# State loop, routing and experts of a two-layer AdaLN kernel: another order, another operand, other loads

## What is computed

```python
def layer0_mixer(u):                         # chunked state space model
    z, x, B, C, dt = split(layer_norm(u) @ in_proj_w.T)
    y = ssd_chunked(x, dA, B, C, chunk) + x * D
    return u + (y * silu(z)) @ out_proj_w.T

def layer0_moe(x):                           # E=64, K=8, CAP=64, H=256, I=96
    w, sel = top_k(softmax(x @ gate_w.T), K) # w is then divided by its sum
    pos = cumsum(one_hot(eid)) ...           # place of a token in its expert
    inp = zeros(E, CAP, H).at[eid, pos].set(x[tok])   # if pos < CAP
    h = silu(inp @ wg) * (inp @ wu)
    out = h @ wd
    return sum over K of out[eid, pos] * w
```

## Time and profile before

| | |
|---|---|
| median of 3 runs | 800.57 us (797.09 to 804.24) |
| the profiled execution, span | 801.1 us |
| busy | PE 77%, DVE 63%, ACT 35%, POOL 31% |
| chain that ended last | PE 53%, DVE 21%, issue 8%, ACT 8%, DMA 6% |
| DMA | 62.83 MB, mean 78 GB/s |

### The profile page before, as it was taken

The page is one execution under the profiler, slowest core; times in us unless marked ns, Lnnn a source line. Parts: engine busy times, 40 slices in busy tenths (PEclk is TensorE's granted clock), DMA queues, the critical chain, the costliest instruction groups (busy, mean ns, idle before and its releaser), DMA issues.

```text
span 801.1 us, 9617 instructions
## 1 busy us (share of the span) xinstructions
PE 620.3 (77%) x3248; PEld 469.8 (59%) x3248; DVE 508.0 (63%) x1121; ACT 283.7 (35%) x887; POOL 249.7 (31%) x288
## 2 busy tenths in 40 slices
PE   2997988740109789975385898898988789998996
PEld 0544766530008677763163665666666668887885
DVE  5547567833997536724677789889757636655444
ACT  2644544400103222332255665646646431111110
POOL 1228003275650000137545255251101126640000
PEclk9999999965559956987577999999999999999999
DMA  8900001049017996863112043150000000000000
GB/s 317 351 1 0 1 2 47 34 147 299 3 42 205 278 281 222 244 195 98 45 48 49 5 54 37 17 53 1 0 1 1 1 0 1 1 1 27 1 1 27
DMA packets 29808, 62.83 MB, mean 78 GB/s; under 512 B 5827, under 2 KB 13297, under 8 KB 29184
## 3 DMA queue, kind: packets, MB, share of 16 engines
q1 hardware_dynamic: 22336, 45.42, 18.1%
q0 software_dynamic: 7424, 16.80, 9.3%
HBM read 48.56 MB, written 17.83 MB: 83 GB/s over the span
## 4 chain that ended last, share of the span: by engine, by line
PE 53%; DVE 21%; issue 8%; ACT 8%; DMA 6%; POOL 2%; another core or an unknown queue 1%; SPq 1%; POOLq 0%; DVEq 0%; ACTq 0%
PE bank L1104 47%; DMA arena<-expert_in 4%; DVE arena L1054 2%; POOL expert_in L396 2%; ACT arena L594 2%; DVE arena L1013 2%; PE bank L1326 2%; PE bank L1444 1%; DVE arena L968 1%; DMA expert_out<-arena 1%; PE bank L1272 1%; ACT arena L612 1%; DMA arena<-in_wmod 1%; DVE arena L1002 1%
## 5 line engine op out<-in xcount | busy, mean ns | idle before, releaser
L1104 PE MATMUL bank<-arena 128*96 128x64 f32 (+9 forms) x2040 | 425.2, 367 | 64.0 <-issue 26.0
L1104 PEld LDWEIGHTS bank<-arena 128*128 128x128 f32 (+4 forms) x2040 | 295.3, 192 | 160.6 <-issue 100.9
L396 POOL DMA_INDIRECT expert_in<-arena x64 | 65.2, 1019 | 88.7 <-DVE arena L857 70.1
L410 POOL DMA_INDIRECT arena<-expert_out,arena x64 | 72.6, 1134 | 19.0 <-issue 18.5
L692 ACT ACTIVATE arena<-bank 128x512 f32<-128x512 f32 x32 | 19.1, 598 | 112.4 <-PE bank L1104 112.4
L1085 DVE TENSOR_TENSOR arena<-arena,bank 128x512 f32<-128x512 f32 x32 | 22.0, 687 | 56.1 <-ACT arena L692 56.1
L594 ACT ACTIVATE arena<-bank,arena 128x128 f32<-128x128 f32 x128 | 45.2, 383 | 25.2 <-DVE arena L1006 25.2
L1104 PE MATMUL bank<-h_hi,gu_hi 128*128 128x512 f32 x128 | 50.8, 397 | 0.5 <-ACT arena L695 0.5
L1104 PE MATMUL bank<-h_low,gu_hi 128*128 128x512 f32 x128 | 50.5, 394 | 0.0
L1104 PE MATMUL bank<-h_hi,low 128*128 128x512 f32 x128 | 50.1, 391 | 0.0
L434 POOL TENSOR_TENSOR low<-arena,gu_hi 128x128 fp32r<-128x128 f32 x64 | 29.7, 495 | 60.4 <-DVE dn_hi L1017 60.4
(11 more groups left out here) (200 smaller groups left out, 1024.2 us busy)
## 6 DMA issues: line engine op xcount, KB each, us to landing
arena<-in_wgu SPq DMA_DIRECT2D x32, 384.0 KB, 6.5
arena<-in_wd SPq DMA_DIRECT2D x32, 192.0 KB, 8.9
expert_in<-arena SPq DMA_DIRECT2D x1, 4096.0 KB, 23.9
arena<-expert_in SPq DMA_DIRECT2D x16, 256.0 KB, 7.2
expert_out<-arena POOLq DMA_DIRECT2D x16, 256.0 KB, 6.5
arena<-in_w SPq DMA_DIRECT2D x1, 2048.0 KB, 9.3
arena<-in_wmod SPq DMA_DIRECT2D x1, 1536.0 KB, 15.0
arena<-in_w_in SPq DMA_DIRECT2D x1, 1288.0 KB, 8.8
```

What stands on the lines that cost most here:

```text
L396: pool.indirect_dma_start(xin, bass.IndirectOffsetOnAxis(scatter8[:, t, k:k + 1], 0), h[:, t, :], None, bounds_check=SLOTS - 1, oob_is_err ...
L410: pool.indirect_dma_start(gath[t % 2][:, k, :], None, yex, bass.IndirectOffsetOnAxis(gather8[:, t, k:k + 1], 0), bounds_check=SLOTS - 1, o ...
L1104: return pe.matmul(o, lhsT, rhs, start=start, stop=stop, **kw)
```

## The change

- **Turns.** The state loop and its routing have T+2 = 10 turns. Turn s routes tile s-2 whole: its transposes stand first in PE's turn (L1257's counterpart), then `cs_rows` and G, then its logits; DVE and ACT take them in the same turn, and the place multiplications close PE's turn, in `bank5`. There are no batches; `choose` and `place_rows` lose the normalisation of the weights, which is done once for all tiles behind the loop.
- **Fewer operations on DVE.** POOL multiplies `w_out` by the gate row once, so x gains tile by tile in one addition. The scale and shift of the experts' input leave DVE: ACT applies them by partition as it copies the transposed tile (two operations) and the transposed expert rows (two a group); four transposes ahead of the loop make the columns (`h2_cols`). What is scattered is the normalised row.
- **Loads.** Pairs 0 to 10 and 12 load one or two a turn inside the loop, as `st_mm` and `yT_mm` reach a turn; pair 11 and one set of codes behind it. z and x of a tile stand side by side so that slots come free. `load_rows` moves from SP's queue to POOL's, between the stores.
- **Experts.** The rows are the stationary side, 64 columns, and gate and up weights, 192 columns, move past them; two experts fill the two halves of a bank's partitions. The hidden tile is then transposed (`hidden_T`, two more transposes a group) and copied by ACT. Three output buffers instead of two, each of 128 partitions, one copy a group.
- **Decoding** a half set of codes takes 4 operations on DVE instead of 7; the pace is 1.5 halves a group instead of 1.25.
- **Gathers.** Two tiles are gathered ahead of the first attention turn instead of three, and behind L425 of tile t stands `gather(t + 2)` instead of `gather(t + 3)`.

```diff
-            for q in range(4):
+            for q, tile, early in ((0, 1, True), (1, 2, True), (2, 2, True), (3, 3, True), (6, 3, True), (12, 4, True), (4, 1, False),
+                                   (5, 2, False), (7, 4, False), (8, 5, False), (9, 6, False), (10, 7, False)):
+                sp.wait_ge(st_mm if early else yT_mm, tile)
                 load_pair(q)
             sp.wait_ge(yT_mm, T)
-            load_codes(0)
-            load_codes(1)
-            for q in range(4, NS):
-                load_pair(q)
-            for n in range(2, NEARLY):
+            load_pair(11)
+            for n in range(NEARLY):
                 load_codes(n)
...
+            pool.wait_ge(ld_wout, 16)
+            pool.tensor_tensor(w_out_s, w_out_s, under(mod[0][:, 2, :], 4), ALU.mult).then_inc(wout_ready, 1)
...
+            def load_rows(g):
+
+                if g >= NX:
+                    pool.wait_ge(xgT_mm, g - NX + 1)
+                pool.dma_start(xg[g % NX], xin[4 * CAP * g:4 * CAP * (g + 1), :].rearrange("(q p) c -> p q c", p=P))\
+                    .then_inc(xg_loaded[g % NX], 16)
+
+            pool.wait_ge(scattered, 16 * T * TOPK)
+            for g in range(NX):
+                load_rows(g)
             for g in range(NG):
...
+                if g + NX < NG:
+                    load_rows(g + NX)
+                pool.wait_ge(ob_ready, g + 1)
+                pool.dma_start(yex[4 * CAP * g:4 * CAP * (g + 1), :].rearrange("(q p) c -> p q c", p=P), ob[g % 3])\
+                    .then_inc(ob_stored[g % 3], 16)
+
+            for i in range(3):
+                pool.wait_ge(ob_stored[i], 16 * len(range(i, NG, 3)))
...
-            for t in range(3):
-                gather(t)
+            gather(0)
+            gather(1)
...
-                if t + 3 < T:
-                    gather(t + 3)
+                if t + 2 < T:
+                    gather(t + 2)
...
-            for s in range(T + 4):
+            for s in range(T + 2):
+                if 0 <= s - 2:
+                    less_maximum(s - 2)
                 if s < T - 1:
                     state_after(s)
-                if 0 <= s - 3 < T:
-                    less_maximum(s - 3)
+                if 0 <= s - 2:
+                    choose(s - 2)
                 if s + 1 < T:
                     make_M(s + 1)
+
+                if 0 <= s - 1 < T:
+                    t = s - 1
+                    dve.wait_ge(o_mm, t + 1)
+                    dve.wait_ge(xh_ready, t + 1)
+                    dve.tensor_tensor(x[:, t, :], x[:, t, :], bank[7][:, 0:DM], ALU.add).then_inc(x1_ready, 1)
+                    dve.wait_ge(x1_ready, t + 1)
+                    moments(x[:, t, :], t, mv[2]).then_inc(var_ready, 1)
 
                 if s < T:
                     dve.wait_ge(Yd_mm, s + 1)
...
                 if 0 <= s - 1 < T:
                     t = s - 1
-                    dve.wait_ge(o_mm, t + 1)
-                    dve.wait_ge(xh_ready, t + 1)
-                    link(dve.tensor_tensor(h[:, t, :], bank[7][:, 0:DM], mod[0][:, 2, :], ALU.mult))
-                    dve.tensor_tensor(x[:, t, :], x[:, t, :], h[:, t, :], ALU.add).then_inc(x1_ready, 1)
-                    dve.wait_ge(x1_ready, t + 1)
-                    moments(x[:, t, :], t, mv[2]).then_inc(var2_ready, 1)
-                if s - 4 in LAST:
-                    place_rows(LAST.index(s - 4))
-                if s - 3 in LAST:
-                    choose(LAST.index(s - 3))
-
-                if 0 <= s - 1 < T:
-                    t = s - 1
-                    dve.wait_ge(rstd2_ready, t + 1)
-                    link(normed(h[:, t, :], x[:, t, :], t, mv[2], rstd[2]))
-                    link(dve.tensor_tensor(h[:, t, :], h[:, t, :], mod[0][:, 4, :], ALU.mult))
-                    dve.tensor_tensor(h[:, t, :], h[:, t, :], mod[0][:, 3, :], ALU.add).then_inc(h2_ready, 1)
-
+                    dve.wait_ge(rstd_ready, 1 + T + t + 1)
+                    normed(h[:, t, :], x[:, t, :], t, mv[2], rstd[2]).then_inc(h2_ready, 1)
+                if 0 <= s - 2:
+                    place_rows(s - 2)
...
+            for s in range(T + 2):
+                if 0 <= s - 2:
+                    t = s - 2
+                    pe.wait_ge(h2_ready, t + 1)
+                    pe.wait_ge(yT_ready, t + 1)
+                    for j in range(KC):
+                        ins = pe.transpose(bank[6][:, j * P:(j + 1) * P], h[:, t, j * P:(j + 1) * P], ident)
+                    ins.then_inc(rowsT_mm, 1)
                 if s + 1 < T:
                     cs_rows(s + 1)
+                    pe.wait_ge(M_ready, s + 1)
+                    mm(bank[2][:, 0:P], bT[:, s + 1, :], cT[:, s + 1, :]).then_inc(G_mm, 1)
+                if 0 <= s - 2:
+                    t = s - 2
+                    if t == 0:
+                        pe.wait_ge(ld_gate, 16)
+                    pe.wait_ge(rowsT_ready, 2 * T + 2 * t + 2)
...
                         pe.wait_ge(xdec_ready, s + 1)
                         if s >= 1:
                             pe.wait_ge(state_ready, s)
+                        if s >= 3:
+                            pe.wait_ge(place_read, s - 2)
                         mm(bank[5][:, :], bn[:, s, :], xdec[s]).then_inc(st_mm, 1)
                     if s >= 1:
                         pe.wait_ge(state_ready, s)
                         if s >= 2:
                             pe.wait_ge(yo_ready, s - 1)
                         mm(bank[4][:, :], cT[:, s, :], state[:, s % 2, :]).then_inc(Yo_mm, 1)
-                    if s >= 1:
-                        pe.wait_ge(y_ready, s)
-                    pe.wait_ge(xD_ready, s + 1)
-                    mm(bank[3][:, :], ident, xD[s], start=True, stop=False, skip_group_check=True)
-                    places(s)
-                    if s + 1 < T:
-                        pe.wait_ge(M_ready, s + 1)
...
-                    pe.wait_ge(M_ready, s + 1)
-                    for i in range(H):
-                        ins = mm(bank[3][:, i * HD:(i + 1) * HD], Lm[:, s % 2, i * P:(i + 1) * P], xs[:, s, i * HD:(i + 1) * HD],
-                                 start=False, stop=True, skip_group_check=True)
-                    ins.then_inc(Yd_mm, 1)
                 if 0 <= s - 1 < T:
                     t = s - 1
                     pe.wait_ge(y_ready, t + 1)
-                    if t >= 2:
-                        pe.wait_ge(h2T_ready, t - 1)
-                        pe.wait_ge(lmax_ready, t - 1)
+                    if t >= 1:
+                        pe.wait_ge(lmax_ready, t)
                     for j in range(4):
                         ins = pe.transpose(bank[6][:, j * P:(j + 1) * P], zs[:, t, j * P:(j + 1) * P], ident)
                     ins.then_inc(yT_mm, 1)
+                if s < T:
+                    pe.wait_ge(xD_ready, s + 1)
+                    mm(bank[3][:, :], ident, xD[s], start=True, stop=False, skip_group_check=True)
+                if 0 <= s - 1 < T:
+                    t = s - 1
                     if t == 0:
-                        pe.wait_ge(ld_wout, 16)
+                        pe.wait_ge(wout_ready, 1)
                     pe.wait_ge(yT_ready, t + 1)
                     if t >= 1:
                         pe.wait_ge(x1_ready, t)
                     for j in range(4):
                         ins = mm(bank[7][:, 0:DM], yT[:, t % 2, j * P:(j + 1) * P], w_out_s[:, j, :], start=j == 0, stop=j == 3)
                     ins.then_inc(o_mm, 1)
-                if 0 <= s - 2 < T:
+                if s < T:
+                    pe.wait_ge(M_ready, s + 1)
+                    for i in range(H):
+                        ins = mm(bank[3][:, i * HD:(i + 1) * HD], Lm[:, s % 2, i * P:(i + 1) * P], xs[:, s, i * HD:(i + 1) * HD],
+                                 start=False, stop=True, skip_group_check=True)
+                    ins.then_inc(Yd_mm, 1)
+                if 0 <= s - 2:
                     t = s - 2
-                    pe.wait_ge(h2_ready, t + 1)
+                    pe.wait_ge(mask_ready, t + 1)
+                    pe.wait_ge(state_ready, min(s + 1, T - 1))
                     if t >= 1:
-                        pe.wait_ge(lmax_ready, t)
...
+                        pe.wait_ge(place_read, t)
+                    mm(bank[5][:, 0:E], strict_b, mask_b[:, t, :], stop=False)
+                    mm(bank[5][:, 0:E], ones_b, run_b[:, t, :], start=False).then_inc(pos_mm, 1)
...
             def gate_up(g):
-                pe.wait_ge(xgT_ready, g + 1)
+                pe.wait_ge(xgT_ready, 2 * (g + 1))
                 if g >= 2:
                     pe.wait_ge(hid_ready, g - 1)
-                for e in range(4):
-                    q = 2 * g + e // 2
-                    if e % 2 == 0:
-                        pe.wait_ge(w_loaded[q % NS], 32 * (q // NS + 1))
-                    w = wgu_s[q % NS][:, e % 2, :].rearrange("p (a j f) -> p a j f", a=2, j=KC)
-                    for a in range(2):
-                        for j in range(KC):
```

(31 more changed lines are left out.)

331 lines of the change are left out of this document (144 added, 187 removed).

## The result

The changed kernel takes 829.76 us in the median (827.72 to 830.09) against 802.4 (four runs of the kernel before): 1.0358 times the time of before, 95% interval 1.0297 to 1.042. It is slower by 3.6%. The forecast was 778, with a range of 755 to 806. The profiled execution spans 827.5 us, 26.4 more than before.

The account below looks back on a forecast made before the run. PE bounds the state loop, one chain through all engines the routing tail, DMA the experts, DVE attention. 801.1 - 33.2 (earlier experts) - 20.9 (experts and output) + 31.9 (attention) = 778.9, less 0.5: 778 us, range 755 to 806.

Parts of the forecast that it names:

- the last takes 1.0, and DVE may start 1.9 later: Attention: gathered rows ready about 14.0 us after the rotary operation starts; DVE's waits cost +31.9 us in all.
- Turn: 11.42 - 1.16 + 1.8 = 12.06 us: State loop: two waits for ACT go, a 1.8 us wait for the norm comes; bounds 11.4 and 12.6.
- the slow rival: State loop: PE's clock falls to half behind the new wait, +10 us a turn, up to 850 us; chance 0.12.
- `Yd` of turn 1: State loop: PE's last long work of turn 1 was to end at 93.9 us, 90.7 in the kernel before.
- I take 5.0: Experts: PE's time per group taken as 5.0 us, 83 us in 16 groups.
- take 86 us: Experts: DMA needs 86 us for the stage's own 25.3 MB at 294 GB/s.
- side by side: Experts: both partition halves run at once, PE's group 2.9 us, stage on the DMA floor, 771 us; chance 0.10.
- lose about 3 us before the first `down` frees slots: Experts: DMA loses about 3 us early in the stage, from its start at 203.
- With 2 us of stalls: Experts: PE ends at 296 with 2 us of stalls, giving a stage of 90.3 us, 17.3 less.
- Rows on POOL's queue: Experts: rows from POOL's queue would overtake weights, so PE's 4.36 us wait would go; the sum did not use it.
- The third output buffer, -3.6: End of experts: the last copy's wait goes; gathers begin 5.3 us after PE's end instead of 8.9.
- two turns less: Tail of routing: one part of the -33.2 us by which the experts start earlier.

Follow-up runs that it names:

- a_one_half: a_swap_e with both experts of a pair written to the same half of the bank's partitions, half the expert outputs missing; 831.34 us, one run.
- a_swap_e: The changed kernel with the two inner loops of gate and up exchanged, both chunks of one expert first; 821.97 us, one run.
- a_codes2: The changed kernel with two sets of codes decoded ahead instead of one and 1.25 half sets a group instead of 1.5; 823.82 us.
- a_codes3: The changed kernel with a third buffer for codes, three sets loaded right behind the loop; 823.84 us.
- a_codes_scratch: a_codes3 with later code sets loaded into a buffer nothing reads, DVE decoding the first two sets again and again; 822.09 us.
- a_late_loads: The changed kernel with all 13 pairs of weights loaded behind the loop in one burst; 830.36 us.
- a_gather3: The changed kernel with three tiles gathered ahead of attention and gather(t + 3) again, as in the kernel before; 769.79 us.
- a_norm_first: The changed kernel with DVE's norm of the routed tile moved ahead of y in each loop turn; 812.60 us.
- a_fill: The changed kernel with five useless multiplications in PE's wait at the head of turns 2 to 7; 820.06 us.
- b_gather2: The kernel before with only the gathers changed: two tiles ahead, gather(t + 2); 862.18 us, 1.083 of before.

## Why the prediction was wrong, step by step

**Attention, "the last takes 1.0, and DVE may start 1.9 later".** The mechanism, the place and the number of turns were right, the term was mis-sized: +52.5 us over the turns instead of 26.8. The rows come 17.6 us after the rotary operation's start (522.61 to 540.24), not 14.0: 2.6 of the 3.6 us are the landing, 4.5 instead of 1.9, and 1.0 is the pace on POOL, 10.6 us from the first gather's start to the last's where the sum had 9.25 and some 0.3 for DVE. Both terms came from the head of attention, where DVE stands idle; they were used in the middle of a turn. The kernel before has that case too, hidden there, since nobody waits for it. Its DMA view from 499 to 509 (a digit for the busy tenths of each quarter microsecond):

```profile
DMA  9018928915918909950692000000000000000000
```

POOL's last gather of that turn starts at 499.92 and takes 1.00, and DMA is busy until 504.5: 3.6 us behind its end, and 16.8 behind L425's start at 487.74. With 16.8 the sum would have had 2.8 us more for each of five turns, 14 of the 25.7. The Trainium skill (Perfetto Trace Analysis, DMA Instruction — SWDGE (GPSIMD)) says that such an instruction ends in the profile when its descriptors are written, not when the data has moved; the rows agree, with 1.9 and 4.5 us between the two. The second part of the miss is PE's clock: behind 10.6 us of idle PE's first four multiplications take 3.75 us at clock 0.50, and POOL's rotary operation starts 17.4 us after `maxima` instead of 16.2; that the one makes the other is argued and not tested. Also, one turn of before was 29.0 us and not 31.2 (the prediction took one for all), which alone is 2 us.

**The loop, "Turn: 11.42 - 1.16 + 1.8 = 12.06 us".** The wait was right within 0.03 us. That the work would then go on at clock 1.00 was the argument against the slow rival ("the loop's clock is 1.00 now, waits included"), and the waits of 0.69 and 0.47 us say nothing of one of 1.77. The rival was priced as all or nothing, at 10 us a turn; what came is 1.6 us a turn in nearly all of them. `Yd` of turn 1 was 3 us late besides (97.2 instead of 93.9): the projections ahead of the loop ran at low clock (3.62 us for four that took 1.88). The last scatter was out at 210.7, not 201.8. The chain behind it (scatter bound by POOL, PE 3.9 us later) was right, with 4.7.

**The experts, "I take 5.0" and "take 86 us".** PE's price was wrong (2.4 us and transposes 1.1), and the rival "side by side" was right about the halves; by a_one_half against a_swap_e this is worth 9 us of the kernel, but the stage did not fall to the DMA floor as that rival had it. DMA's own term was right: 26.0 MB at 300 GB/s are 87 us. The step that failed is "lose about 3 us before the first `down` frees slots" and "With 2 us of stalls". DMA is idle 12.9 us in the stage: some 5 at its start (share 0.49 in the first ten) and the rest where DVE waits for codes, PE for DVE, and SP for PE's slots. That the hidden tile stands behind the decoding on DVE, and the decoding behind a load, was not looked at. The number of sets decoded ahead, one instead of two, is not to blame (a_codes2, with two sets and the old pace: 26 us of waits for the hidden tile against 23); a_codes3 and a_codes_scratch put the price of waiting for codes at 6 to 8 us of the kernel.

**Rows on POOL's queue.** The sum did not rest on it, and rightly: PE still waits 3.61 and 4.07 us for rows (4.36 in the earlier trace rows). The rule cited from the Trainium skill (DMA: Bandwidth & Descriptors, Queues, rings and completion order) let one expect the wait to go; this case doesn't bear that out. Rows land 7.9 us after their issue in the median, 7.2 from SP's queue before, and both loads that PE waited for (issued at 225.64 and 276.74) stood in POOL's queue behind a store that had waited 7.42 and 11.20 us for ACT, which the sum did not look at. No run here undid the move alone, so what it is worth stays open.

**The third output buffer, -3.6.** The gathers begin 9.6 us after PE's end, not 5.3. ACT's last copy comes 1.5 us behind PE's end where it came 3.7 behind, but it still waits 2.62 us for an older store:

```profile
316.40 0.60 ACT L578 ACTIVATE arena<-bank 128x512 f32<-128x512 f32 x1 [2.62 <-DMA expert_out<-arena]
```

and POOL waits another 5.71 us for the last store to land, where it had stood idle 2.37 before. The same 256 KB land 6.4 us after their issue and took 2.9 before: from 317 to 324.5 another 1.05 MB, attention weights, are on DMA, and beside the last store of before there was nothing. The sum took the wait for the older store as all that stood there; another buffer doesn't change when a store lands.

**Right** were two turns less as a saving in the tail (its other half, the weights out of the tail, was worth nothing: a_late_loads), that the loads in the loop cost nothing, and the way from first gather to first `maxima` (58.1 against 60.4).

## What to carry to other kernels

A wait on the engine that sets the pace costs more than its length if its clock falls behind it: find what can stand in it, or what releases it earlier. How long a transfer takes is read where it will run, from the DMA view, and not from POOL's row or a quiet place. A stage whose DMA share is near 1 is priced by its bytes first; here 34 us of PE's work were worth 9. And where one trace gives a strange gap, a second trace of the same code is the cheapest test of it.

## What the runs showed of the hardware

- Behind 1.77 us of idle PE the granted clock was at 0.50 for 3.4 us (112.0 to 115.4), in most turns and not in all (a_gather3 at 111.28); behind waits of 0.41 us (a_norm_first, 92 to 150) and with useless work in the wait (a_fill, 105 to 165) it stayed at 1.00.
- Two multiplications with 64 stationary columns, in different halves of the output partitions, overlap almost wholly: 24 in 2.4 us, against 4.54 us in one half, all at clock 1.00; two orders of the pairs gave 2.38 and 2.44.
- Gathers in the middle of an attention turn land 3.6 to 4.5 us after POOL's instruction, at the head of the stage 1.9. The DMA engines are busy longer for the same bytes: 45% of 20 us for 1.05 MB (522 to 542) against 31% of 21 us for 1.89 MB (324 to 345), 2.5 times as long for each. Why isn't settled: no experiment was made for it.
- Two executions of the same code can differ: DVE's small operations under the burst of weights were 1.4 us apart in the trace of before and 0.25 in b_gather2's; in the experts' last stretch the same 88 PE instructions took 11.18 us in the one and 20.63 in the other.
